# Expert stage of a four-part layer: where the picks are turned, where tile 1 is compared, and how the ranking is dealt over a turn

## The chip, the cores and the metric

The program runs on one core of one Trainium2 chip. The metric is device time in microseconds (us) for one execution. A profiled execution leaves a trace of every instruction on TensorE (PE, with its weight loads as PEld), VectorE (DVE), ScalarE (ACT), GpSimd (POOL) and SyncE (SP). Times in rows count from the start of the profiled span.

## The reference

The input x is 4 batches of 512 tokens of width 256. Four residual updates follow each other: a cross attention with a bias, an attention with gated expert values, a cross attention with layer norm, and a product-key expert layer. The change sits at the seam between the third and the fourth, and in the fourth. Cut to what matters, the fourth is:

```python
def _L1_ffn_ref(x, w_q, keys, expert_down, expert_up, norm_w):      # H=8, DK=128, K=8, NKEYS=64
    xn = _rmsnorm(x, norm_w)
    q = (xn @ w_q.T).reshape(b, t, H, 2, DK)
    sim1 = einsum('bthd,hkd->bthk', q[..., 0, :], keys[:, :, 0, :])
    sim2 = einsum('bthd,hkd->bthk', q[..., 1, :], keys[:, :, 1, :])
    s1, i1 = top_k(sim1, K); s2, i2 = top_k(sim2, K)
    all_idx = i1[..., :, None] * NKEYS + i2[..., None, :]
    all_sc  = s1[..., :, None] + s2[..., None, :]
    fs, pk = top_k(all_sc, K)                                        # 8 heads x 8 picks = 64 picks a token
    fi = take_along_axis(all_idx, pk)
    hidden = gelu(einsum('btd,bthkd->bthk', xn, expert_down[fi])) * relu(fs)
    return einsum('bthk,bthkd->btd', hidden, expert_up[fi])
```

## The kernel before

The kernel is four program blocks, one for each part of the layer. All engines meet at the end of a block, and the next begins when the last of them is done. Inside a block each engine has its own hand-written order of work, and semaphores tie them together.

The expert block (`product_key_experts`) takes the 2048 tokens as 16 tiles of 128. It gathers nothing: all 4096 experts are computed densely, as 128 x 32. For a tile there are these steps.

- ACT normalises the tile (`stage_tile`), PE turns it (`turn_x`, L2379), and ACT takes it out (L2486).
- PE compares it with the folded keys: 8 matmuls of 512 columns (`compare`, L2390). ACT takes the similarities out (`sims`, L2493).
- DVE ranks them in parts. Part 0 is 16 MAX8 (`largest`, L2186) and part 1 the 16 places (`largest_places`, L2282). Parts 2 to 5 (`rank`, L2235 to L2272) add pairs, take the 8 best of each head and work out the expert's row and column.
- PE turns the picks (`turn_picks`, L2400, 12 small matmuls), ACT takes them out (`picks`, L2500 and L2501), and DVE splits the score (`split_score`, L2553 and L2556) into three bf16 parts.
- DVE builds one-hots for the 64 picks in four rounds of 16 (`onehots`, rounds 0 to 3, L2569, L2574, L2580). There are two buffers for them.
- PE computes the hidden values of all experts in 8 blocks of 16 matmuls (`hidden`, L2416), and ACT applies gelu to each (L2509).
- PE sums the one-hots into a dense matrix of weights in 8 blocks of 24 matmuls (`weights`, L2433). DVE multiplies it with the hidden values (`apply`, L2592).
- PE multiplies the product with the up table in 8 blocks of 8 matmuls (`spend`, L2443). DVE adds the result to x (`update`, L2598).

The work is software-pipelined. Turn i runs over blocks n = 0 to 7. In each block PE does `spend` of tile i-1, `hidden` of tile i+1 and `weights` of tile i. In turn i the similarities of tile i+2 are made too, after block 3, and the picks of tile i+1 are turned in block 5. DVE does `apply(i, n)` in each block. Beside it come, in blocks 0 to 3, the ranking of tile i+1 (parts 1, 2, 3, then 4 and 5 together), the last two one-hot rounds of tile i in blocks 1 and 3, MAX8 of tile i+2 in block 5, the split and round 0 of tile i+1 in block 6, and its round 1 in block 7. From turn 2 on, block 4 also holds a small part of a late norm.

PE's waits in a turn are these. `weights(i, n)` with even n waits for one-hot round n/2 of tile i, and from n = 3 on for `apply(i, n-3)`, since three PSUM banks go round. `spend(i-1, 0)` of the next turn waits for the last `apply`. `turn_picks(i+1)` waits for the 43rd ranking step.

Before turn 0, the expert block runs `hidden(0, 2)` to `hidden(0, 7)`, with `turn_x(1)` after the first, `turn_picks(0)` after block 4 and `compare(1)` at the end. Blocks 0 and 1, and the ranking of tile 0, already ran in the attention block before it. Then PE waits for the up table (4 MB, issued by SP at the block's start behind 1 MB of the down table) and for both halves of tile 1's similarities:

```python
                compare(1, 1)
                eng.wait_ge(s["up_loaded"], 16)
                eng.wait_ge(sim_ready.sem, sim_ready.at(1, 2))
```

At the end of the attention block, PE projects four query tiles (L520) and DVE adds each to x (`update`, two instructions, L766 and L769). The fourth goes through PSUM bank 6.

## Time and profile before

| What | Value |
|---|---|
| Median of 3 runs | 2230.97 us (2230.22 to 2232.72) |
| Profiled execution: its own time | 2233.26 us |
| Profiled execution: span | 2231.5 us |
| Mean granted TensorE clock | 0.997 |
| PE busy | 2169.8 us, 97% |
| DVE busy | 1686.2 us, 76% |
| ACT busy | 814.7 us, 37% |
| POOL busy | 177.8 us, 8% |

A row of a timeline gives the start, the duration, the engine, the line, the operation and how many instructions are merged. In brackets stands the engine's idle time before it and what ended that. PE durations are modelled a little long: in a chain without a gap the next group starts about 0.16 us before the printed end. The profiled execution took 2.3 us more than the median of the runs. 1.8 us of its time lie outside the span.

### The profile page before, as it was taken

To read this page: it belongs to the slowest core of one execution; us is meant where nothing else is said; L and a number is where in the kernel's file an instruction comes from. 1 tells how busy PE (TensorE), PEld (TensorE's weight loads), DVE (VectorE), ACT (ScalarE), POOL (GpSimd) and SP (SyncE) were. 2 spreads that over 40 slices of the span, in tenths; PEclk is the share of its full clock that TensorE was granted. 3 is DMA by queue.
4 is the path that set the end of the run, shared out by engine and by line. 5 is a ranking of instruction groups with operands and counts; after the bars stand their busy time and mean duration, and the time that the engine had idled before them with its cause. 6 is when DMAs were issued, how large, how long until landed. Compare 5 with 4: busy or idle time off the path is not lost. (4 is left out here: it accounts for less than half of the span.)

```text
span 2231.5 us, 45916 instructions
## 1 busy us (share of the span) xinstructions
PE 2169.8 (97%) x18243; PEld 1464.3 (66%) x18276; DVE 1686.2 (76%) x4495; ACT 814.7 (37%) x1943; POOL 177.8 (8%) x427
## 2 busy tenths in 40 slices
PE   7999999999999999999999999999989999999998
PEld 3555554446756756775555555556679989898997
DVE  6898896876576576536877787877698989888885
ACT  4888882311312302303554554545322111211110
POOL 4552201000000000000000000000000000000000
PEclk9999999999999999999999999999999999999999
DMA  5011104000000003001000000001200000000000
GB/s 179 24 42 44 28 9 156 1 1 1 1 1 1 1 0 114 1 1 50 2 1 1 1 1 1 1 1 58 95 1 2 2 11 2 1 11 2 1 11 11
DMA packets 24166, 48.65 MB, mean 22 GB/s; under 512 B 5009, under 2 KB 13457, under 8 KB 22929
## 3 DMA queue, kind: packets, MB, share of 16 engines
q1 hardware_dynamic: 23952, 45.71, 6.2%
q8 instruction: 146, 2.39, 0.4%
q14 instruction: 68, 0.55, 0.1%
HBM read 37.57 MB, written 2.10 MB: 18 GB/s over the span
## 5 line engine op out<-in xcount | busy, mean ns | idle before, releaser
L2416 PE MATMUL banks<-work,big 128*128 128x128 f32 x2016 | 248.9, 277 | 2.2 <-PEq L378 1.5
L623 ACT ACTIVATE work<-banks,work 128x512 f32<-128x512 f32 x256 | 174.6, 686 | 202.3 <-DVE work L742 202.3
L2416 PEld LDWEIGHTS banks<-work,big 128*128 128x128 f32 x2016 | 242.3, 193 | 7.8 <-issue 3.4
L1121 PE MATMUL banks<-big,work 128*128 128x256 f32 x1024 | 241.3, 379 | 3.6 <-issue 3.3
L1045 PE MATMUL banks<-big,work 128*128 128x512 f32 x512 | 226.6, 596 | 0.3 <-DMA big<-in_B_val 0.2
L2509 ACT ACTIVATE work<-banks 128x512 f32<-128x512 f32 x126 | 75.2, 597 | 407.4 <-PE banks L2416 404.3
L1121 PEld LDWEIGHTS banks<-big,work 128*128 128x128 f32 x1024 | 195.4, 191 | 33.6 <-issue 1.9
L1939 ACT ACTIVATE work<-work 128x512 f32<-128x512 f32 x256 | 181.0, 711 | 0.0
L1045 PEld LDWEIGHTS banks<-big,work 128*128 128x128 f32 x512 | 95.6, 190 | 114.0 <-issue 112.6
L742 DVE TENSOR_REDUCE work<-banks 128x2 f32<-128x1024 f32 x128 | 150.5, 1218 | 7.7 <-PE banks L475 7.7
L1343 DVE CUSTOM_DVE_ANT_0 work<-banks,work 128x512 f32<-128x512 f32 (+3 forms) x128 | 57.7, 488 | 121.5 <-PE banks L1061 109.2
L1843 PEld LDWEIGHTS banks<-ident,work 64*128 64x128 f32 x2048 | 75.5, 139 | 90.9 <-ACT work L1939 58.7
L1228 ACT ACTIVATE work<-work 128x512 f32<-128x512 f32 (+3 forms) x128 | 70.8, 554 | 168.7 <-DVE work L1343 168.7
L491 PEld LDWEIGHTS banks<-ident,work 64*128 64x128 f32 x2048 | 74.0, 139 | 89.0 <-issue 51.5
L2443 PE MATMUL banks<-big,wab 128*128 128x256 f32 x512 | 126.4, 390 | 3.6 <-DVE wab L2592 3.6
L1312 DVE TENSOR_TENSOR work<-banks,work 128x512 f32<-128x512 f32 x128 | 88.0, 691 | 51.8 <-PE banks L1045 51.3
L475 PE MATMUL banks<-work 64*128 64x256 f32 x1024 | 124.6, 383 | 0.9 <-DVE work L735 0.9
L2443 PE MATMUL banks<-big,work 128*128 128x256 f32 x512 | 123.7, 387 | 0.8 <-DVE work L2592 0.8
L504 PE MATMUL banks<-big,wc 128*64 128x512 f32 x512 | 116.9, 599 | 3.2 <-ACT wc L644 2.9
L760 DVE COPY big<-banks 128x512 f32<-128x512 f32 x128 | 87.7, 685 | 38.9 <-PE banks L491 38.7
L751 DVE TENSOR_SCALAR work<-work 128x512 f32<-128x512 f32 x256 | 113.1, 484 | 4.5
L2433 PEld LDWEIGHTS banks<-wc 128*128 128x128 bf16 x3072 | 107.2, 99 | 13.5 <-issue 5.4
(252 smaller groups left out, 3801.3 us busy)
## 6 DMA issues: line engine op xcount, KB each, us to landing
work<-work SPq DMA_DIRECT2D x152, 32.0 KB, 2.0
big<-in_bias SPq DMA_DIRECT2D x16, 256.0 KB, 4.7
big<-in_B_val SPq DMA_DIRECT2D x8, 512.0 KB, 6.6
big<-in_B_out SPq DMA_DIRECT2D x1, 4096.0 KB, 18.3
big<-in_D_downT SPq DMA_DIRECT2D x4, 1024.0 KB, 5.0
big<-in_D_up SPq DMA_DIRECT2D x1, 4096.0 KB, 15.7
wc<-in_ctxT SPq DMA_DIRECT2D x1, 2048.0 KB, 7.8
wab<-in_L_ffn_w_q SPq DMA_DIRECT2D x1, 2048.0 KB, 9.7
```

The lines of the kernel that those rows point to most:

```text
L475: last = eng.matmul(SB[i][:, j, c * 256:(c + 1) * 256], qT[r, t % 2, qt * P:(qt + 1) * P], kT[r, t % 2, c * 256:(c + 1) * 256], start=True ...
L504: last = eng.matmul(FB[0][j * DK:(j + 1) * DK, :], vtok[:, kt, h * DK:(h + 1) * DK], pT[:, (t % 2 * PAIR + j) * QT + kt, :], start=(kt == ...
L623: eng.activation(prob[:, n % NS * PAIR + j, :], SB[n % 2][:, j, :], ACT.Exp, bias=low[:, n % NS, j:j + 1], accum_out=rowsum[:, n % NS, j:j ...
L742: eng.tensor_reduce(low[:, n % NS, :], SB[n % 2], AX.X, ALU.max, negate=True).then_inc(low_ready.sem, 1)
L751: last = eng.tensor_scalar(one, one, rinv[:, n % NS, j:j + 1], None, ALU.mult)
L1045: last = eng.matmul(value_bank(b, n), xnT[:, kc, t * P:(t + 1) * P], w_val[:, kc, h * EB * DK:(h + 1) * EB * DK], start=(kc == 0), stop=(k ...
L1121: last = eng.matmul(XO[qt // 2][:, qt % 2 * D:(qt % 2 + 1) * D], spread[:, c % NG, qt * P:(qt + 1) * P], w_out[:, c, :], start=False, stop ...
L1312: eng.tensor_tensor(scaled[:, n % NG, :].rearrange("p (k e) -> p k e", e=EB), value_bank(b, n).rearrange("p (k e) -> p k e", e=EB), gm[:, ...
L1939: eng.activation(one, one, ACT.Exp, bias=low[:, n % 2, j:j + 1], scale=-1.0, accum_out=rowsum[:, n // QT % 2, at:at + 1]).then_inc(p_ready, 1)
L2416: last = eng.matmul(HP[n % 2][:, q * P:(q + 1) * P], down[:, (n * NJ + q) * KC + kc, :], xnT[par][:, kc, :], start=(kc == 0), stop=(kc == ...
L2433: last = eng.matmul(dst, hot[:, c, at, :], lot[c][:, at, f, :], start=(f == 0), stop=(f == 2))
L2443: last = eng.matmul(UPP[par][:, 0:D], G[par][:, j, :], up[:, j, :], start=(j == 0), stop=(j == ELO - 1))
```

## The change

In the attention block:

- the fourth `update` leaves DVE's order, and ACT's order ends with `stage_tile(1)`, which used to be ACT's first work in the expert block.

In the expert block, before turn 0:

- PE begins with `turn_picks(0)` and ACT with `picks(0)`;
- `turn_x(1)` stays after `hidden(0, 2)`, and now waits until ACT has taken the picks out;
- `compare(1)` comes after `hidden(0, 4)` and writes banks 2 and 3 in place of 0 and 1, without waiting for a gelu;
- DVE begins with the attention's fourth update (`last_update`), then split and one-hot rounds 0 and 1 of tile 0, then ranking parts 0 and 1 of tile 1.

In the turns:

- `turn_picks(i+1)` and `picks(i+1)` go from block 5 to block 7;
- `weights(i, 0)` is issued in block 1, behind `hidden(i+1, 1)` and right before `weights(i, 1)`;
- the ranking of tile i+1 is dealt as parts 1, 2, 3 in blocks 0, 1, 2, part 4 in block 4 and part 5 in block 5 (in turn 0, where part 1 is done: parts 2, 3, 4, 5 in blocks 0, 2, 4, 5);
- MAX8 of tile i+2 goes from block 5 to 6; the split and both one-hot rounds of tile i+1 come together after `apply(i, 7)`.

```diff
@@ c_attention
                 start_gelu(eng, m, 1)
+                stage_tile(eng, m, 1)
...
                 update(B - 1, 2, FB[1])
-                update(B - 1, 3, FB[0])
@@ product_key_experts, tensor
                     eng.wait_ge(staged.sem, staged.at(i, 1))
+                    if i == 1:
+                        eng.wait_ge(selt_ready.sem, selt_ready.at(0, 2))
...
-                    if i:
-                        before = (i - 1, SELECT + 1) if i >= 2 else (0, NB)
-                        eng.wait_ge(h_ready.sem, h_ready.at(*before))
+                    if i >= 2:
+                        eng.wait_ge(h_ready.sem, h_ready.at(i - 1, SELECT + 1))
...
+                turn_picks(0)
                 for n in range(2, NB):
                     hidden(0, 0, n)
                     if n == 2:
                         turn_x(1)
-                    if n == START_PICK:
-                        turn_picks(0)
-                compare(1, 1)
+                    if n == SELECT + 1:
+                        compare(1, 1)
...
                         if n == PICK and ahead >= 1:      # PICK 5 -> 7
                             turn_picks(i + 1)
-                        if n != SELECT + 1:
+                        if n == 1:
+                            weights(i, 0)
+                        if n and n != SELECT + 1:
                             weights(i, n)
@@ scalar
-                stage_tile(eng, m, 1)
+                picks(0)
                 for n in range(2, NB):
                     hidden(0, 0, n)
-                    if n == START_PICK:
-                        picks(0)
-                select(1, 1)
+                    if n == 2:
+                        take_x(1, 1)
+                    if n == SELECT + 1:
+                        take_sims(1)
@@ vector
+                def last_update():
+                    eng.wait_ge(c_out.sem, c_out.at(B - 1, QT))
+                    eng.tensor_tensor(c_y, bank[6][:, 0:D], c_bo, ALU.add).then_inc(c_added, 1)
+                    eng.wait_ge(c_added, 1)
+                    xt = x[:, NT - 1, :]
+                    eng.scalar_tensor_tensor(out=xt, in0=c_y, scalar=m["gates"][:, 5:6], in1=xt, op0=ALU.mult, op1=ALU.add
+                                             ).then_inc(c_added, 1)
+                last_update()
                 split_score(0)
                 onehots(0, 0)
                 onehots(0, 1)
                 topk(1, 0)
+                topk(1, 1)
+                PARTS = {0: 1, 1: 2, 2: 3, 4: 4, 5: 5}
+                FIRST_PARTS = {0: 2, 2: 3, 4: 4, 5: 5}
...
-                        if ahead >= 1 and n < 4:
-                            topk(i + 1, n + 1)
+                        parts = PARTS if i else FIRST_PARTS
+                        if ahead >= 1 and n in parts:
+                            topk(i + 1, parts[n])
...
-                        if ahead >= 2 and n == PICK:
+                        if ahead >= 2 and n == PICK - 1:
                             topk(i + 2, 0)
-                        if ahead >= 1 and n == PICK + 1:
+                        if ahead >= 1 and n == PICK:
                             split_score(i + 1)
                             onehots(i + 1, 0)
-                        if ahead >= 1 and n == NB - 1:
                             onehots(i + 1, 1)
```

## Rows read from the trace of the kernel before

**Rows 1.** Windows: length, busy (count) of PE, PEld, DVE, ACT, POOL; PEclk, DMA, GB/s.

```profile
1636.00:1648.00 12.00, 8.66 (x123) 8.57 (x124) 9.37 (x36) 2.18 (x5) 0.00 (x0) 0.86 0.00 1
...
1687.00:1726.00 39.00, 39.00 (x414) 34.84 (x413) 34.44 (x125) 7.50 (x15) 0.00 (x0) 1.00 0.01 2
...
2190.00:2198.00 8.00, 6.19 (x48) 5.22 (x49) 5.85 (x6) 0.00 (x0) 0.00 (x0) 0.79 0.01 2
```

**Rows 2.** PE's waits in the expert stage: us in total, times, longest.

```profile
PE banks L2400 <- DVE work L2272: 5.3, 2, 4.2
PE banks L2443 <- DVE wab L2592: 3.6, 2, 1.9
```

**Rows 3.** Timeline of PE, from the block's start to turn 0.

```profile
1598.18 2.02 PE L2416 MATMUL banks<-work,big 128*128 128x128 f32 x16 [1.45 <-PEq L378]
...
1603.92 0.57 PE L2400 MATMUL banks<-ident,work 128*64 128x64 f32 x12
1604.43 5.62 PE L2416 MATMUL banks<-work,big 128*128 128x128 f32 x48
1611.26 3.70 PE L2390 MATMUL banks<-work 128*128 128x512 f32 x8 [1.20 <-ACT work L2486]
1615.69 2.02 PE L2416 MATMUL banks<-work,big 128*128 128x128 f32 x16 [0.73 <-issue]
```

**Rows 4.** Timeline of PE, end of turn 0 and start of turn 1.

```profile
1639.34 0.57 PE L2400 MATMUL banks<-ident,work 128*64 128x64 f32 x12 [4.20 <-DVE work L2272]
...
1647.23 2.03 PE L2416 MATMUL banks<-work,big 128*128 128x128 f32 x16
1650.97 2.00 PE L2443 MATMUL banks<-big,wab 128*128 128x256 f32 x8 [1.71 <-DVE wab L2592]
```

**Rows 5.** Timeline of PE, three groups of a later turn.

```profile
1689.78 2.00 PE L2443 MATMUL banks<-big,work 128*128 128x256 f32 x8
1691.61 0.86 PE L2433 MATMUL banks<-wc 128*128 128x64 bf16 x24
1692.31 1.97 PE L2443 MATMUL banks<-big,work 128*128 128x256 f32 x8
```

**Rows 6.** Timeline of PE, turns 14 and 15.

```profile
2179.99 0.57 PE L2400 MATMUL banks<-ident,work 128*64 128x64 f32 x12 [1.05 <-DVE work L2272]
...
2191.81 2.91 PE L2443 MATMUL banks<-big,wab 128*128 128x256 f32 x8 [1.85 <-DVE wab L2592]
...
2212.84 0.86 PE L2433 MATMUL banks<-wc 128*128 128x64 bf16 x24
2214.48 14.08 PE L2443 MATMUL banks<-big,work 128*128 128x256 f32 x64 [0.78 <-DVE work L2592]
```

**Rows 7.** Timeline of DVE, from the last update of the attention block on.

```profile
1597.23 0.48 DVE L769 SCALAR_TENSOR_TENSOR x<-work,gates,x 128x256 f32<-128x256 f32 x1
1605.17 0.23 DVE L2553 CAST work<-work 128x128 bf16<-128x128 f32 x1 [7.46 <-ACT work L2501]
...
1606.53 0.69 DVE L2569 TENSOR_TENSOR wc<-work,wc 128x1024 bf16<-128x1024 bf16 x1
...
1609.94 0.69 DVE L2569 TENSOR_TENSOR wc<-work,wc 128x1024 bf16<-128x1024 bf16 x1
...
1626.25 0.68 DVE L2235 TENSOR_TENSOR wab<-work 128x512 f32<-128x512 f32 x1
...
1635.02 0.42 DVE L2223 TENSOR_TENSOR wab<-work 128x512 bf16<-128x512 bf16 x1
...
1639.19 0.68 DVE L2592 TENSOR_TENSOR wab<-banks,work 128x512 f32<-128x512 f32 x1
...
1642.09 1.98 DVE L2186 MAX8 work<-work 128x8 f32<-128x64 f32 x15
```

**Rows 8.** Timeline of SP: the up table's issue.

```profile
1598.36 0.42 SPq L2355 DMA_DIRECT2D big<-in_D_up  x1
```

**Rows 9.** DMA issues of that stretch: KB, us from issue to landing.

```profile
big<-in_D_up SPq DMA_DIRECT2D x1, 4096.0 KB, 15.7
```

More of the change, by code:

```diff
@@ L145, in build @@
         m["A.dve_took"] = sem("A_dve_took")
+        m["C.out_made"] = Signal(nc, ctx, "C_out_made", QT)
         m["B.spent"] = Signal(nc, ctx, "B_spread_used", B_.groups * EB)
@@ L365, in c_attention @@
         av_made, on_ready = sig("av_made", T), sig("onorm_ready", T)
-        out_made, y_ready, turn_done = sig("out_made", QT), sig("y_ready", QT), sig("x_updated", QT)
+        out_made, y_ready, turn_done = m["C.out_made"], sig("y_ready", QT), sig("x_updated", QT)
         norm, e = m["C.norm"], m["D"]
@@ L2322, in product_key_experts @@
     gate = m["gates"][:, 3:4]
+    c_out, c_y, c_bo = m["C.out_made"], m["work"][:, 15616:15872], m["work"][:, 15872:16128]
     every_other = ident.rearrange("p (n two) -> p two n", two=2)
-    SELECT, PICK, START_PICK = 3, 5, 4
+    SELECT, PICK = 3, 7
     late, LATE, LATE_FROM = e.norm, 4, 2
@@ L2332, in sem @@
             return ctx.enter_context(nc.semaphore("D_" + what))
-        consts = sem("consts")
+        consts, c_added = sem("consts"), sem("last_attention_added")
         staged, xt_made, xt_ready, sim_made, sim_ready, step = e.staged, e.xt_made, e.xt_ready, e.sim_made, e.sim_ready, e.step
@@ L2384, in compare @@
                     eng.wait_ge(xt_ready.sem, xt_ready.at(i, 1))
-                    if i:
-                        before = (i - 1, SELECT + 1) if i >= 2 else (0, NB)
-                        eng.wait_ge(h_ready.sem, h_ready.at(*before))
+                    if i >= 2:
+                        eng.wait_ge(h_ready.sem, h_ready.at(i - 1, SELECT + 1))
                     for n in range(2):
                         for kc in range(KC):
-                            last = eng.matmul(HP[n][:, :], xnT[par][:, kc, :], simw[:, kc, n * 512:(n + 1) * 512],
+                            last = eng.matmul(WP[n] if i == 1 else HP[n][:, :], xnT[par][:, kc, :], simw[:, kc, n * 512:(n + 1) * 512],
                                               start=(kc == 0), stop=(kc == KC - 1))
@@ L2482, in _, with take_x @@
             def _(eng):
-                def select(i, par):
+                def take_x(i, par):
                     eng.wait_ge(xt_made.sem, xt_made.at(i, 1))
@@ L2488, in select, with take_sims @@
                     last.then_inc(xt_ready.sem, 1)
+                def take_sims(i):
                     for n in range(2):
@@ L2493, in select @@
                         eng.activation(sims[:, n * HD:(n + 1) * HD, :],
-                                       HP[n][:, :].rearrange("p (a b) -> p a b", b=NK), ACT.Copy).then_inc(sim_ready.sem, 1)
+                                       (WP[n] if i == 1 else HP[n][:, :]).rearrange("p (a b) -> p a b", b=NK), ACT.Copy).then_inc(sim_ready.sem, 1)
                 def picks(i):
@@ L2525, in turn @@
                         if ahead >= 2 and n == SELECT:
-                            select(i + 2, par)
+                            take_x(i + 2, par)
+                            take_sims(i + 2)
                         if ahead >= 1 and n == PICK:
@@ L2545, in topk @@
                         rank(eng, m, i, part, selt_made)
-                    if part == 4:
-                        rank(eng, m, i, 5, selt_made)
                 def split_score(i):
@@ L2612, in turn @@
                             update(i - 2, par)
-                        if ahead >= 1 and n < 4:
-                            topk(i + 1, n + 1)
+                        parts = PARTS if i else FIRST_PARTS
+                        if ahead >= 1 and n in parts:
+                            topk(i + 1, parts[n])
                         if n == LATE and LATE_FROM <= i < LATE_FROM + late.parts:
+                            if i == LATE_FROM:
+                                eng.wait_ge(c_added, 2)
                             late.on_vector(eng, B - 1, i - LATE_FROM)
-                        if ahead >= 2 and n == PICK:
+                        if ahead >= 2 and n == PICK - 1:
                             topk(i + 2, 0)
-                        if ahead >= 1 and n == PICK + 1:
+                        if ahead >= 1 and n == PICK:
                             split_score(i + 1)
                             onehots(i + 1, 0)
-                        if ahead >= 1 and n == NB - 1:
                             onehots(i + 1, 1)
```

## The prediction

> **What bounds the kernel now.** I read the windows first. In a whole steady turn PE is busy for 39.00 of 39.00 us at clock 1.00, while DVE is busy for 34.44 us [rows 1]. So the turns from 1 to 13 are bound by PE, and moving work among DVE's slots there can gain nothing. It can only lose. The change removes no matmul. What it can win is idle PE time, so the next view is PE's waits, and there only the first and the last turns count: the picks waited for ranking (L2400 for DVE L2272) 5.3 us in two places, and the first `spend` of a turn for `apply` 3.6 us in two places [rows 2]. The timeline places them: 4.20 us before the picks of tile 1 and 1.71 us before the first `spend` of turn 1 [rows 4], 1.05 and 1.85 us in turns 14 and 15 [rows 6]. At the block's start there are three more: 1.45 us between the blocks, 1.20 us before `compare(1)` and 0.73 us before turn 0 [rows 3].
>
> Two of these waits cost more than their length. Around the 4.20 us the granted clock averaged 0.86 over 12 us, so part of it ran at 1.2 instead of 2.4 GHz: 0.14 x 12 = 1.7 us lost. Around the 1.85 us it was 0.79 over 8 us: another 1.7 us [rows 1, 6]. After 1.71 us idle the `spend` took 2.00 us [rows 4], as in a turn without a wait [rows 5], so that one cost only itself.
>
> **Block start.** The attention block now ends with PE, not with DVE's fourth update. DVE ended at 1597.23 + 0.48 = 1597.71, and PE began 0.47 us later, at 1598.18 [rows 3, 7]. PE itself had ended at 1598.18 - 1.45 = 1596.73 [rows 3]. With the same 0.47 us the stage starts at 1597.2, 1.0 us earlier. The two instructions of the update (about 1 us) now lie on DVE at the block's start, where DVE was idle for 7.46 us [rows 7]. `stage_tile(1)` lies on ACT, idle during the last projections. Both cost nothing.
>
> **From there to turn 0.** PE issues the picks (0.51 us, from 1603.92 to 1604.43), then blocks 2 to 4 with `turn_x` in between (5.74 us, from 1598.18 to 1603.92), `compare(1)` (3.70 us printed, less the 0.16 us by which groups overlap: 3.54), then blocks 5 to 7 (5.62 less 0.16, about 5.5) [rows 3]. The new wait of `turn_x(1)` for ACT's copies is covered by `hidden(0, 2)`, 1.87 us against about 0.6 us of copies behind the picks; behind it would queue only PE. `compare(1)` has `hidden(0, 3)` and `hidden(0, 4)` between it and ACT's copy, so the 1.20 us wait goes, and blocks 5 to 7 lie between it and turn 0, so the 0.73 us goes. PE is through at 1597.2 + 0.51 + 5.74 + 3.54 + 5.5 = 1612.5.
>
> What is late next is the up table. Its DMA was issued at 1598.36 and took 15.7 us [rows 8, 9]: landed at 1614.1, hidden behind the wait that ended at 1615.69. Issued 1.0 us earlier, it lands at 1613.1. Its cost is a wait of 0.6 us. So turn 0 begins at 1613.1 against 1615.69 [rows 3]: **gain 2.6 us**. Bounds: 3.2 if the table is not late, 1.6 if it lands no earlier than before.
>
> The Trainium skill, "DMA: Bandwidth & Descriptors", section "Measured", gives 341 GB/s for 1 MB and 425 GB/s for 16 MB, issued from GpSimd. An estimate from it for the two transfers, 5.2 MB at some 400 GB/s, is 13 us: the table would be in time, and the total would be 0.6 us better. The row says 15.7 us, and I go by the row.
>
> **Turn 0.** It lasted 1647.23 - 1615.69 = 31.54 us [rows 3, 4]. Without the 4.20 us wait and the 1.7 us of slow clock it is 25.6 us. The question is whether DVE now delivers the picks by then. PE reaches them, before `weights(0, 7)`, at 25.6 - 0.51 - 0.70 = 24.4 us into the turn. DVE enters the turn with parts 0 and 1 of tile 1 done: the last one-hot round of tile 0 ends near 1597.2 + 1.2 (copies) + 1.36 + 2 x 3.41 = 1606.6; tile 1's similarities are there near 1607.9, and parts 0 and 1 take 2.1 and about 3.1 us, to 1613.2, before the first `apply` can start. That is what the move of `compare(1)` buys. `apply(0, 0)` starts behind two hidden blocks and one block of weights, 2 x 1.87 + 0.86 + 0.1 = 4.7 us in. From there to the end of part 5 there are parts 4 and 5, 1639.19 - 1635.02 = 4.17 us; parts 2 and 3, which are the 8.77 us from 1626.25 to 1635.02 less two `apply` of 0.68 and one one-hot round of 3.41, 4.00 us; two one-hot rounds, 6.82 us; and six `apply`, 4.1 us [rows 7]. Sum 19.1, so the picks are ready 23.8 us in, 0.6 us before PE asks. The 4.20 us and its clock loss go: **gain 5.9 us**. The margin is thin: beyond it each us late costs one.
>
> **Start of turn 1.** `spend(0, 0)` needs `apply(0, 7)`. DVE has `apply(0, 6)` and the MAX8s of tile 2 (about 2.1 us [rows 7]) in front: 23.8 + 0.7 + 2.1 + 0.7 = 27.3 us into turn 0. PE gets there at 25.6 + 1.87 = 27.5. The 1.71 us go [rows 4]: **gain 1.7 us**. Before, a split and one-hot round lay in front of that `apply`; they now lie behind it.
>
> **The steady turns.** No gain, and a cost of nothing if the new chain fits. Let P be the start of `turn_picks(i+1)`. `weights(i, 7)` starts at P + 0.51, and `apply(i, 7)` ends at about P + 2.1 (0.51, then 1.64 us from a block of weights to the `spend` behind its `apply` [rows 6]). Split and one-hot round 0 then take 1.36 + 3.41 [rows 7]: ready at P + 6.9. PE asks for it in `weights(i+1, 0)`, behind `weights(i, 7)`, two hidden and two spend blocks: P + 0.51 + 0.70 + 2 x 1.87 + 2 x 1.83 = P + 8.6 [rows 3, 5]. Slack 1.7 us. Moving `weights(., 0)` back by one block makes that slack; without it there would be none. DVE's extra work in turns 2 to 9 (a part of the norm) falls in block 4, before it waits for block 5. Ranking ends some 4 us before the picks, as the turn has 4.5 us of free DVE time [rows 1].
>
> **Turns 14 and 15.** Turn 14 has no compare and so asks for the picks 3.5 us sooner, but block 7 is two blocks later than block 5: the 1.05 us go. In turn 15 there are no hidden blocks to hide the chain. After `weights(14, 7)` the first `spend` waits 0.8 us, as the last one does [rows 6], against 1.85. Then `spend(14, 0)` and `(14, 1)` end at P + 2.1 + 2 x 1.83 = P + 5.8, and `weights(15, 0)` waits until P + 6.9: a new wait of 1.1 us. `weights(15, 2)` waits for round 1 (3.41 us later, P + 10.3) and PE is there at P + 6.9 + 1.4 + 1.83 = P + 10.1: 0.2 us. New waits 2.1, old 1.05 + 1.85 + 1.7 of slow clock = 4.6: **gain 2.5 us**, if the clock holds.
>
> The row of 1.85 us idle shows a fall of the clock, that of 1.71 us none [rows 4, 6]. Here there are three short waits close together, and whether they count as one, no row says. Bounds: 0 and 1.7 us. I take 0, because none is longer than 1.71 us. The Trainium skill, "TensorE: Matmul & The Clock Gate", section "What's actually happening", says that the clock follows how busy TensorE has been recently, with the slow state as the default. That speaks against the change at this place: by it the scattered waits could add up to the same fall, and the total gain would be 11.0 us instead of 12.7.
>
> **Sum.** 2.6 + 5.9 + 1.7 + 2.5 = 12.7 us. Of the profiled execution, 2233.26 us, that leaves 2220.6; it stands 2.3 us above the median of the runs, so for the median 2230.97 - 12.7 = **2218.3 us**, 0.57% faster.
>
> **Rivals.**
>
> - *The change works, but part is given back:* the clock falls in turn 15 (1.7 us), or the thin margins of 0.6 us in turn 0 and 0.2 us in turn 1 are missed by 1 to 3 us. For it speaks that both margins are smaller than what I had to estimate without a row (ACT's copies, waking times). 2220 to 2224 us.
> - *Turn 0 stays bound by DVE:* if DVE could not use the earlier start (parts 0 and 1 not done before the first `apply`), the picks wait and the `spend` wait come back. Only the block start and the end are left, 5.1 us: 2225.9. Against it: the 7.46 us in which DVE was idle before the split [rows 7], and now fills.
> - *A wait in every turn, and slower:* the one-hots of the next tile start only after `apply(i, 7)`, and the first weights of each turn stand behind them. If that chain (picks, ACT, DVE, weights) is later than I count by more than its slack of 1.7 us, each further us costs 15 us over 15 turns. From 2.5 us late on it eats the whole gain; at 3.5 us late it gives 2230.97 - 12.7 + 15 x 1.8 = 2245 us. For it: DVE has three more things in a row there than before. Against it: every duration in the chain is from a row, and none varies.
> - *Nothing changes:* the waits only move, to the up table or to the attention block's end. The table would have to land 5 us later than before to take even half of the gain, and nothing is put in front of it. 2229 to 2232 us.
>
> **How the numbers follow.** My forecast, 2216 to 2220 us, has a chance of 0.68; the first rival 0.18; DVE-bound turn 0 0.04; a wait in every turn 0.07, of which 0.05 ends slower; nothing 0.03. About 0.2% (4.5 us) is what a measurement of this kernel can tell from no change, so faster means under 2226.5: 0.68 + 0.18 + 0.04 = 0.90, same 0.05, slower 0.05. The range takes in the forecast with its bounds (0.6 better with the table in time, 1 for the spread of runs) and the first rival: 2216 to 2223.
>
> **What would show it.** In the profile after: PE's first group near 1597.2 and it is the picks; turn 0 starts near 1613.1, behind a short wait for a DMA; no wait of PE for L2272 anywhere; turn 0 of 25.6 us; steady turns without a gap in PE, as before; in turn 15 waits of about 0.8, 1.1 and 0.2 us, and the clock there near 1.00. A wait of `weights` for the one-hot rounds (L2580) in each turn, or gaps of PE in the steady turns, would make the forecast wrong.

## The result, and the profile after

The changed kernel takes 2214.26 us (median of 4 runs, 2212.79 to 2215.63). Beside it the kernel before took 2230.59 us (4 runs, 2230.01 to 2232.72). The ratio is 0.9925, with an interval of 0.9908 to 0.9942: 16.3 us faster. The direction was as forecast, the size was not. The forecast was 2218.3 us, 12.7 us less, and its range began at 2216, 1.7 us above the measured median. The same change, timed again beside the experiments of the third batch, gave 0.9919 (0.9905 to 0.9932). By both intervals the gain is more than the 12.7 us forecast (0.9942 of 2230.59 us is 12.9 us less).

The profiled execution of the changed kernel took 2212.79 us with a span of 2211.0 us, 20.5 us less than the span before. Of these, 3.0 us arise ahead of the expert stage, in parts that the change doesn't touch: in the profiles of this study the projections of the attention block end anywhere from 1593.7 to 1598.5 us. I therefore compare stage with stage, from the end of PE's last projection (start of PE's first group in the expert block less the idle time printed there) to the start of the last 64 `spend` matmuls. Before that is 1596.73 to 2214.48 [rows 3, 6], 617.75 us. After it is 1593.73 to 2193.99, 600.26 us. The gain inside the stage is **17.5 us**. Behind it lie 17.0 us in both.

The timeline of PE after, from the block's start to the second block of turn 1:

```profile
1594.05 0.57 PE L2403 MATMUL banks<-ident,work 128*64 128x64 f32 x12 [0.32 <-PEq L379]
1594.55 2.05 PE L2419 MATMUL banks<-work,big 128*128 128x128 f32 x16
...
1600.23 3.60 PE L2393 MATMUL banks<-work 128*128 128x512 f32 x8
1603.66 5.52 PE L2419 MATMUL banks<-work,big 128*128 128x128 f32 x48
1609.84 3.84 PE L2419 MATMUL banks<-work,big 128*128 128x128 f32 x32 [0.66 <-DMA big<-in_D_up]
...
1634.30 0.57 PE L2403 MATMUL banks<-ident,work 128*64 128x64 f32 x12
1634.81 0.87 PE L2436 MATMUL banks<-wc 128*128 128x64 bf16 x24
1635.52 2.03 PE L2419 MATMUL banks<-work,big 128*128 128x128 f32 x16
1637.38 3.62 PE L2446 MATMUL banks<-big,wab 128*128 128x256 f32 x16
```

The same view at turn 2, turns 13 and 14, and the end:

```profile
1674.00 2.03 PE L2419 MATMUL banks<-work,big 128*128 128x128 f32 x16
1675.87 3.62 PE L2446 MATMUL banks<-big,work 128*128 128x256 f32 x16
...
2097.32 2.03 PE L2419 MATMUL banks<-work,big 128*128 128x128 f32 x16
...
2135.80 2.03 PE L2419 MATMUL banks<-work,big 128*128 128x128 f32 x16
...
2171.63 3.72 PE L2446 MATMUL banks<-big,wab 128*128 128x256 f32 x16 [0.78 <-DVE wab L2599]
...
2176.38 1.57 PE L2436 MATMUL banks<-wc 128*128 128x64 bf16 x48 [1.03 <-DVE wc L2587]
...
2193.99 14.08 PE L2446 MATMUL banks<-big,work 128*128 128x256 f32 x64 [0.78 <-DVE work L2599]
```

All waits of PE in the expert stage after (us in total, times, longest), against the long ones of [rows 2]:

```profile
PE banks L2436 <- DVE wc L2587: 1.0, 1, 1.0
PE banks L2446 <- DVE wab L2599: 0.8, 1, 0.8
PE banks L2446 <- DVE work L2599: 0.8, 1, 0.8
PE banks L2393 <- ACT work L2491: 0.7, 1, 0.7
PE banks L2419 <- DMA big<-in_D_up: 0.7, 1, 0.7
PE banks L2403 <- PEq L379: 0.3, 1, 0.3
```

The reader is to see three things. The picks (L2403) at 1634.30 and the first `spend` at 1637.38 have no bracket any more. A new short bracket stands ahead of turn 0, for the up table. And from one turn's start to the next, 2097.32 to 2135.80, there are 38.48 us, where a turn before took 38.81 (1687.77 to 1726.58 in the rows of the next section). The stage, split at the same points in both traces (turns counted from their first `hidden` group):

| Stretch | before, us | after, us | gain | forecast |
|---|---|---|---|---|
| Projections' end to turn 0 | 18.96 | 16.11 | 2.85 | 2.6 |
| Turn 0 | 31.54 | 25.68 | 5.86 | 5.9 |
| Turn 1, its start to its first `spend` | 3.74 | 1.86 | 1.88 | 1.7 |
| From there to the start of turn 14 | 502.51 | 498.42 | **4.09** | **0** |
| Turn 14 to the last `spend` | 61.00 | 58.19 | 2.81 | 2.5 |
| Sum | 617.75 | 600.26 | 17.49 | 12.7 |

Four terms are within about 0.3 us of their forecast. The whole miss is one row: 13 steady turns, for which the prediction said "No gain".

### The profile page after: what moved, and what is told of

The parts are those of the page before. It is cut to its first block and busy times, and to the rows that moved or that the text cites. A ratio compares the mean times of both kernels' runs of the same rounds, so it can differ in the third digit from the quotient of the medians.

```text
span 2211.0 us, 45960 instructions
## 1 busy us (share of the span) xinstructions
PE 2163.5 (98%) x18276; PEld 1457.6 (66%) x18276; DVE 1685.3 (76%) x4495; ACT 815.0 (37%) x1943; POOL 178.9 (8%) x427
## 5 line engine op out<-in xcount | busy, mean ns | idle before, releaser
L2587 DVE TENSOR_TENSOR wc<-wc,work 128x3072 bf16<-128x3072 bf16 x64 | 112.1, 1751 | 0.0
## 6 DMA issues: line engine op xcount, KB each, us to landing
big<-in_D_up SPq DMA_DIRECT2D x1, 4096.0 KB, 15.4
```

The lines of the kernel that those rows point to most:

```text
L2587: eng.tensor_tensor(lot[b].rearrange("p n f (j two) -> p n f j two", two=2), elo[:, b].rearrange("p n (j two) -> p n j two", two=2).unsque ...
```

## Why the steady turns became shorter

Before, PE had no printed idle time in a steady turn [rows 1], and [rows 5] show none ahead of the first `spend`. But a `hidden` group and that `spend` started 2.01 us apart before and 1.86 us after. The weight loads of the kernel before, at that same `spend`, tell why. First three of PE's rows of the kernel before, then its weight loads (PEld), then DVE:

```profile
1687.77 2.03 PE L2416 MATMUL banks<-work,big 128*128 128x128 f32 x16
...
1713.17 1.89 PE L2443 MATMUL banks<-big,work 128*128 128x256 f32 x8
...
1726.58 2.03 PE L2416 MATMUL banks<-work,big 128*128 128x128 f32 x16
```

```profile
1689.78 1.59 PEld L2443 LDWEIGHTS banks<-big,work 128*128 128x128 f32 x8 [0.17 <-DVE work L2592]
...
1692.28 1.60 PEld L2443 LDWEIGHTS banks<-big,work 128*128 128x128 f32 x8
```

```profile
1689.04 0.69 DVE L2592 TENSOR_TENSOR work<-banks,work 128x512 f32<-128x512 f32 x1
```

The last `apply` of the turn ended at 1689.04 + 0.69 = 1689.73, and 0.05 us later PE loaded the weights that `apply` had made. The load waited 0.17 us, and the matmul that follows it started in the same instant, 1689.78 [rows 5]. As the printed ends of matmuls are modelled about 0.16 us late, that wait disappears in PE's own rows: the engine is printed as 100% busy. One sign is left in PE's rows: this `spend` is printed with 2.00 us [rows 5], where one behind a `hidden` group, with no wait, is printed with 1.89 (1713.17 above). After the change the loads run ahead of the matmul, as they do elsewhere. PEld and DVE after:

```profile
1675.76 3.33 PEld L2446 LDWEIGHTS banks<-big,work 128*128 128x128 f32 x16
```

```profile
1674.20 0.69 DVE L2599 TENSOR_TENSOR work<-banks,work 128x512 f32<-128x512 f32 x1 [2.17 <-PE banks L2436]
```

`apply` ends at 1674.89, the load starts at 1675.76, and the matmul at 1675.87, 0.11 us behind its load. The wait is worth 0.15 us (2.01 less 1.86), and the first `spend` behind it, whose loads had no lead, took 1.83 against 1.73 us: 0.10. Together 0.25 us a turn. The reason is DVE's order: before, the split and round 0 stood ahead of `apply(i, 7)`; now they stand behind it.

The other 0.08 us of the 0.33: `weights(i, 0)` and `weights(i, 1)` now follow each other, so PE goes 7 times a turn from a bf16 `weights` group to an fp32 group, not 8. In the trace after, `hidden` behind `weights` takes 1.86 us to the next group (2.03 printed), behind `spend` 1.78 (1.95 printed). These are two readings of a trace; experiments 2, 3 and 9 test them.

The experiments below call this 0.08 us a change from bf16 to fp32, but the rows of the loads point to something else: it too is a load that starts late. Behind `weights` the load of an fp32 group starts 0.03 us ahead of its matmul (1692.28 above, for the `spend` at 1692.31 in [rows 5]), behind `hidden` 0.11 us ahead. A `spend` then takes 1.81 or 1.73 us to the next group: 0.08 us less lead, 0.08 us more time. The two leads are each the length of one matmul of the group before, 0.70 / 24 = 0.03 us for `weights` and 1.78 / 16 = 0.11 us for `hidden`. And there is a loss without a change of type: in the kernel before, the fp32 `hidden` matmuls behind the fp32 picks (1604.43) have a load that starts in the same instant, and 48 of them are printed with 5.62 us [rows 3]; after, behind `compare`, 48 are printed with 5.52 us (1603.66 above), both at clock 1.00:

```profile
1604.43 5.44 PEld L2416 LDWEIGHTS banks<-work,big 128*128 128x128 f32 x48
```

All bf16 groups of this kernel are also those with the short matmuls of 64 columns, so no run here separates the type from the length.

## The experiments

Ten kernels, and the change once more, were run in three batches. Each batch had its own runs of the kernel before: 2230.39, 2230.68 and 2231.83 us. "Stage" is the length defined above; the change has 600.3 in both of its profiles. Line numbers shift by a few between the kernels. The stage is read from one profile of each kernel; it repeats well, with 600.26, 600.31, 600.35 and 600.32 us for the change, its second profile and the kernels of experiments 5 and 8. The medians of whole executions are coarser: each interval is about 3 us wide to either side, and the change itself was timed beside the third batch only. So differences of 1 to 2 us among the kernels below rest on the stage.

**1. `weights(i, 0)` back in block 0.**

```diff
-                        if n == 1:
-                            weights(i, 0)
-                        if n and n != SELECT + 1:
+                        if n != SELECT + 1:
                             weights(i, n)
```

> The changed kernel with one thing undone: weights(i, 0) is issued in block 0 of each turn again, behind the first spend, and not in block 1. Theory 1 (the chain picks, ACT's copies, split, one-hot round 0 is ready 6.85 us after the picks start, as the trace of the changed kernel shows, and PE asks for it there): PE would ask 0.51 + 0.71 + 1.86 + 1.73 = 4.8 us after the picks start, so each turn from 1 to 14 gains a wait of about 2.05 us before weights(i, 0) for L2587, the steady turn goes from 38.49 to about 40.6 us, and the time to about 2214 + 14 x 2.1 = 2243 us, slower than the kernel before. Theory 2 (DVE has free time in a turn and catches up, so the order on PE is indifferent): within 2 us of the changed kernel, 2212 to 2217 us.

Measured: 2253.55 us (2250.68 to 2254.55), ratio 1.0104 (1.0088 to 1.0119): slower. The waits of PE, and one of the places in its timeline:

```profile
PE banks L2436 <- DVE wc L2585: 30.0, 15, 2.8
```

```profile
1761.65 1.89 PE L2446 MATMUL banks<-big,work 128*128 128x256 f32 x8
1765.48 0.87 PE L2436 MATMUL banks<-wc 128*128 128x64 bf16 x24 [1.94 <-DVE wc L2585]
1766.19 1.97 PE L2446 MATMUL banks<-big,work 128*128 128x256 f32 x8
```

It is the wait that the third rival of the prediction described, 15 times, and issuing `weights(i, 0)` one block later is what avoids it: the stage is 637.7 us here, 37.4 longer. The time is more than theory 1 gave. A turn without a fall of the clock takes 40.68 us, 2.20 more than 38.48 where about 2.1 was expected: 1.94 printed, 0.16 by which printed idle time is short, and one more change from bf16 to fp32. In three of the turns the granted clock fell after the wait (0.96 mean over the 41 us of one such turn, about 1.6 us lost), in the other turns an equal wait left it at 1.00; and the wait of turn 15 was 2.76 us, longer than any of these and without a fall (clock 1.00 over the 10 us around it).

**2. Split before the last `apply`.** `split_score(i + 1)` ahead of `apply(i, 7)`, which puts about 1.4 us of DVE back before it.

```diff
                     for n in range(NB):
+                        if ahead >= 1 and n == PICK:
+                            split_score(i + 1)
                         apply(i, par, n)
...
                         if ahead >= 1 and n == PICK:
-                            split_score(i + 1)
                             onehots(i + 1, 0)
```

> The changed kernel with the split of the score put before the last apply of each turn on DVE, so that this apply ends about 1.4 us later. Theory 1 (in the kernel before, the first spend of every turn waited for that apply, about 0.15 to 0.25 us, though no gap is printed): the apply now ends near P + 3.24 (P the start of the picks) and the spend, free to start at P + 3.08, starts near P + 3.3; the steady turn goes from 38.49 to 38.7 to 38.8 us, close to the 38.81 of the kernel before, and the time rises by 3 to 5 us. Theory 2 (the 0.33 us a turn come only from the two blocks of weights standing side by side, and no wait is hidden): the steady turn stays at 38.49 us and the time rises by under 1 us, in turn 0 alone.

Measured: 2217.74 us (2214.81 to 2218.51), ratio 0.9939 (0.9926 to 0.9953); stage 602.3, 2.0 longer. From turn 1's first `spend` to turn 14 it takes 500.29 us against 498.42, 0.14 a turn; the first `spend` of turn 1 comes 0.45 later, and turns 14 and 15 give 0.26 back. Again PE prints no gap, and again the loads show it (PE, PEld, DVE of this kernel):

```profile
1674.80 2.03 PE L2419 MATMUL banks<-work,big 128*128 128x128 f32 x16
1676.71 3.72 PE L2446 MATMUL banks<-big,work 128*128 128x256 f32 x16
```

```profile
1676.71 3.32 PEld L2446 LDWEIGHTS banks<-big,work 128*128 128x128 f32 x16
```

```profile
1675.97 0.68 DVE L2599 TENSOR_TENSOR work<-banks,work 128x512 f32<-128x512 f32 x1
```

`apply` ends at 1676.65, load and matmul both start at 1676.71, 0.06 later. The `spend` starts 1.91 us behind the `hidden` where it was 1.86, and the two blocks of `spend` take 3.56 instead of 3.46. A load that loses its lead costs 0.10 even where the matmul itself is only 0.05 late. Theory 1 holds, in a smaller size, since `apply` ends a little earlier here than before the change: 1.85 us behind the start of the `hidden` group, against 1.96. This experiment brings back 0.14 of the 0.25 us; the other 0.11 are read from those 1.96 us and were not put back by a run.

**3. The two weight blocks apart.** `weights(i, 1)` behind `spend(i-1, 2)`, so 8 changes from bf16 to fp32 in a turn again.

```diff
                         if i:
                             spend(i - 1, 1 - par, n)
+                        if n == 2:
+                            weights(i, 1)
...
-                        if n and n != SELECT + 1:
+                        if n > 1 and n != SELECT + 1:
                             weights(i, n)
```

> The changed kernel with weights(i, 1) moved behind spend(i-1, 2), so that the two blocks of weights are no longer side by side, while the first spend and the first weights stay where they are. Theory 1 (most of the 0.33 us a turn is a hidden wait of the first spend, only about 0.08 us is the change between fp32 and bf16 matmuls): steady turn about 38.57 us, time up by about 1 us. Theory 2 (the 0.33 us are all from standing side by side): steady turn about 38.8 us, time up by 4 to 5 us.

Measured: 2217.01 us (2213.92 to 2217.23), ratio 0.9935 (0.9922 to 0.9949); stage 601.4, 1.2 longer. The steady part takes 499.50 us, 0.083 a turn more. That is the 0.08 of theory 1, and with the 0.25 read above it makes up the 0.33.

**4. The seam undone.** The fourth `update` and `stage_tile(1)` at their old places.

```diff
                 start_gelu(eng, m, 1)
-                stage_tile(eng, m, 1)
...
                 update(B - 1, 2, FB[1])
+                update(B - 1, 3, FB[0])
...
+                stage_tile(eng, m, 1)
                 picks(0)
...
-                last_update()
                 split_score(0)
```

> The changed kernel with the seam undone: the attention's fourth update is again DVE's last work in the attention block, and stage_tile(1) is ACT's first in the expert block. Theory 1 (the block starts when its last engine is done, and the up table then bounds the start of turn 0): the expert block starts 1.0 us later after PE's last projection, turn 0 too, and the time rises by about 1.0 us. Since turn_x(1) waits for staging and for the picks' copies, nothing else moves. Theory 2 (the update hides, as its cost is taken from the waits before turn 0): the wait for the up table shrinks and the time stays within 0.3 us.

Measured: 2215.91 us (2212.47 to 2216.65), ratio 0.993 (0.9916 to 0.9943); stage 601.3, 1.0 longer. PE's first row:

```profile
1597.86 0.57 PE L2403 MATMUL banks<-ident,work 128*64 128x64 f32 x12 [1.30 <-PEq L379]
```

1.30 us between the blocks where the change has 0.32: the 1.0 us of the prediction. The wait for the table stays at 0.7, since its issue moves along with the block's start.

**5. `compare(1)` late.** At its old place behind `hidden(0, 7)`, and ACT's `take_sims(1)` with it; the banks as in the change.

```diff
                 for n in range(2, NB):
                     hidden(0, 0, n)
                     if n == 2:
                         turn_x(1)
-                    if n == SELECT + 1:
-                        compare(1, 1)
+                compare(1, 1)
```

> The changed kernel with compare(1) put back to the end of the block's start, behind hidden(0, 7), still in banks 2 and 3. Theory 1 (the early comparison buys almost nothing where it stands: PE waits for the up table anyway, and DVE can use its similarities only to be 0.6 us ahead of the first apply): PE's order is as long as before, the similarities are there about when the up table is, MAX8 and places end 0.6 us after the first apply could start, the picks still come in time, and the time is that of the changed kernel within 0.5 us. Theory 2, that of the prediction (the move of compare(1) is what lets DVE deliver the picks in time): a wait for L2273 before the picks of tile 1 comes back, 2 us or more, with a fall of the clock, and the time rises by 2 to 6 us.

Measured: 2213.71 us (2212.81 to 2215.02), ratio 0.9925 (0.9912 to 0.9939); stage 600.35, the same. In DVE's timeline here tile 1's first MAX8 comes 5.3 us later than in the change (1604.50 there), and the first `apply` 0.6 us later (1614.49 there, behind 4.62 us idle):

```profile
1609.79 0.22 DVE L2187 MAX8 work<-work 128x8 f32<-128x64 f32 x1 [6.32 <-issue]
...
1615.07 0.67 DVE L2597 TENSOR_TENSOR wab<-banks,work 128x512 f32<-128x512 f32 x1
```

Even so the picks come at 1634.32 without a wait. That part of the change buys nothing here, where PE waits for the up table ahead of turn 0 in any case (0.75 us).

**6. The whole block start undone, the turns as in the change.** Experiment 4, and the order of PE, ACT and DVE before turn 0 as before, with all five ranking parts in turn 0.

```diff
-                turn_picks(0)
                 for n in range(2, NB):
                     hidden(0, 0, n)
                     if n == 2:
                         turn_x(1)
-                    if n == SELECT + 1:
-                        compare(1, 1)
+                    if n == 4:
+                        turn_picks(0)
+                compare(1, 1)
...
-                topk(1, 1)
-                FIRST_PARTS = {0: 2, 2: 3, 4: 4, 5: 5}
+                FIRST_PARTS = PARTS
```

> The changed kernel with the whole block start as in the kernel before (fourth update and staging at their old places, picks of tile 0 after block 4, compare(1) last, ranking part 1 of tile 1 inside turn 0); the turns are those of the change. Theory 1 (the stage is the sum of its parts): 2.85 us from the start, and in turn 0 DVE has 3.1 us more to do, so that the picks come about 26.5 us into the turn against 24.4: a wait of about 2.1 us, 0.3 us at the next spend, and perhaps 1.6 us of half clock. Time 5 to 7 us above the changed kernel, about 2219 to 2221 us; steady turn 38.49 us. Theory 2 (the later picks and weights alone remove the waits of turn 0): 2.9 us above. Theory 3 (the waits of turn 0 come back in full): 10 us above.

Measured: 2222.30 us (2219.12 to 2222.74), ratio 0.996 (0.9946 to 0.9973); stage 605.6, 5.3 longer. So the edits in the turns alone bring 12.2 of the 17.5 us, and those at the start, on top of them, 5.3: 2.85 ahead of turn 0, 2.2 for the picks in turn 0, and 0.3 behind them. PE at the picks of tile 1, and the window around them:

```profile
1643.62 0.57 PE L2402 MATMUL banks<-ident,work 128*64 128x64 f32 x12 [2.13 <-DVE work L2273]
```

```profile
1634.00:1650.00 16.00, 13.87 (x169) 13.05 (x168) 15.55 (x46) 3.97 (x8) 0.00 (x0) 1.00 0.01 2
```

2.13 us idle, and the granted clock (1.00, the column behind POOL's) stayed at 2.4 GHz.

**7. Half of the up table early.** 2 MB of the table are issued in the attention block, behind the last but one head pair's product (the expectation says sixth-last, which is a slip), and 2 MB at the expert block's start. `turn_x` and `take_x` in the turns go one block earlier.

```diff
+                eng.wait_ge(av_made.sem, av_made.at(B - 1, T - 1))
+                eng.dma_start(d_views(m)[2][:, :ELO // 2, :], a["D.up"][:, :ELO // 2, :]).then_inc(s["up_loaded"], 16)
...
-                        if n == SELECT and ahead >= 2:
+                        if n == SELECT - 1 and ahead >= 2:
                             turn_x(i + 2)
```

> The changed kernel with two things added: the first half of the up table (2 MB) is fetched from the attention block as soon as its half of the buffer is free, behind the sixth-last head pair's product, and turn_x(i+2) with ACT's copy stands one block earlier in a turn. Theory 1 (the two waits that the trace of the changed kernel still shows at these places, 0.66 us for the table and 0.72 us before compare(2), are real and nothing is late behind them until 1.3 us): both waits go, the picks and the first spend of turn 1 become late by 0.1 to 0.2 us, and the time falls by 1.1 to 1.5 us. Theory 2 (DVE's margins in turn 0, 0.97 us before the picks, take it back): the time falls by under 0.7 us.

Measured: 2213.31 us (2211.36 to 2214.52), ratio 0.992 (0.9906 to 0.9933); stage 598.7, 1.6 shorter, and both waits of 0.7 us (the table, and `compare` in turn 0 for ACT) are gone from the list. The two halves took 8.7 us each to land (median):

```profile
big<-in_D_up SPq DMA_DIRECT2D x2, 2048.0 KB, 8.7
```

**8. Ranking not dealt.** Parts 1, 2, 3 and 4 with 5 in blocks 0 to 3, as before the change.

```diff
-                PARTS = {0: 1, 1: 2, 2: 3, 4: 4, 5: 5}
-                FIRST_PARTS = {0: 2, 2: 3, 4: 4, 5: 5}
+                PARTS = {0: 1, 1: 2, 2: 3, 3: 4}
+                FIRST_PARTS = {1: 2, 2: 3, 3: 4}
...
                         rank(eng, m, i, part, selt_made)
+                    if part == 4:
+                        rank(eng, m, i, 5, selt_made)
```

> The changed kernel with the ranking dealt as before: parts 1, 2, 3, then 4 and 5 together, in blocks 0 to 3 (in turn 0 parts 2, 3, then 4 and 5, in blocks 1 to 3). Theory 1 (with the picks in block 7, DVE's order between the applies has slack, and dealing the ranking over the blocks does nothing): no new wait, time within 0.5 us of the changed kernel. Theory 2 (parts 4 and 5 together hold up apply(i, 4), and weights of blocks 6 and 7 wait for it): a wait of PE for L2599 in each turn, some 1 us each, 10 us or more in all.

Measured: 2213.59 us (2213.13 to 2217.56), ratio 0.9923 (0.9909 to 0.9936); stage 600.3, the same waits. Dealing the ranking over the blocks does nothing here.

**The change again.** The kernel of the change as it stands, as the mark for the third batch.

> The changed kernel once more, for the comparison with the next two in one set of runs. By all theories: 2213 to 2215 us, steady turn 38.49 us, and 600.3 us from the end of the last projection to the start of the last spend.

Measured: 2213.68 us (2212.66 to 2215.89), ratio 0.9919 (0.9905 to 0.9932); stage 600.3.

**9. All blocks of a turn in pairs.** PE's order in a turn: two `spend`, two `hidden`, two `weights`, so 4 changes from bf16 to fp32 instead of 7. Ranking part 4 goes to block 3 and MAX8 to block 5, to fit.

```diff
-                    for n in range(NB):
...
+                    for n in range(0, NB, 2):
+                        if i:
+                            spend(i - 1, 1 - par, n)
+                        if n == SELECT + 1 and ahead >= 2:
+                            compare(i + 2, par)
+                        if i:
+                            spend(i - 1, 1 - par, n + 1)
+                        if n and ahead >= 1:
+                            hidden(i + 1, 1 - par, n)
+                        if ahead >= 1:
+                            hidden(i + 1, 1 - par, n + 1)
+                        weights(i, n)
+                        weights(i, n + 1)
```

> The changed kernel with all blocks of a turn taken in pairs on PE (two spends, two hidden, two weights; the comparison between the spends of blocks 4 and 5), ranking part 4 in block 3 and MAX8 in block 5 so that DVE is in time. Theory 1 (each change from bf16 to fp32 matmuls costs PE 0.08 us, and three more of them go in each turn): steady turn 38.49 - 0.25 = 38.24 us, and the time falls by 3 to 3.6 us. Theory 2 (the 0.08 us belong to the first pair alone, or the gain returns as waits for apply or for one-hot rounds, which now come later by a block): steady turn 38.4 us or more, the time within 1 us or above.

Measured: 2211.89 us (2208.88 to 2213.13), ratio 0.9906 (0.9891 to 0.9921); stage 596.5, 3.8 shorter. A turn of it, from start to start:

```profile
1638.80 2.03 PE L2419 MATMUL banks<-work,big 128*128 128x128 f32 x16
...
1677.04 2.03 PE L2419 MATMUL banks<-work,big 128*128 128x128 f32 x16
```

38.24 us, 0.24 less than 38.48: three changes of 0.08. Of the 3.8 us, 3.2 lie in the steady turns and 0.7 in the last two. The median fell by 1.8 us only, where 3 to 3.6 were expected; in the profile, the part ahead of the stage ended 2.3 us later than in that of the change beside it, and the stage is what the edit acts on.

**10. Pairs, and half of the table early.** Experiments 7 and 9 together; the diff is that of both, with one difference: `turn_x` stands between the two `hidden` groups of a pair.

> The pairs of blocks together with the early half of the up table and the earlier turn_x. Theory 1 (the gains add until DVE bounds turn 0): steady turn 38.24 us; the waits for the table and before compare(2) are gone, and the picks of tile 1 wait about 0.7 us; time 4 to 4.7 us below the changed kernel, about 2209.5 us. Theory 2 (in turn 0 DVE takes all of it back): 3 us below, as the pairs alone.

Measured: 2209.21 us (2208.20 to 2210.97), ratio 0.9899 (0.9884 to 0.9914); stage 595.9. It beats both kernels: 22.6 us under the kernel before and 4.5 us under the change, of the same batch. The two gains don't add up in full (4.4 us against 1.6 + 3.8). About half of what is missing lies in the steady turns: they take 38.29 us, and not the 38.24 that was expected. In experiment 9 the short `turn_x` stands behind `weights` and loses 0.03 us there, and the `spend` behind it loses nothing; here the `spend` stands behind `weights` and loses 0.08. The other half, 0.4 us, lies ahead of turn 1, where a wait of the picks comes back, because turn 0 now starts earlier than DVE can follow:

```profile
1633.15 0.57 PE L2405 MATMUL banks<-ident,work 128*64 128x64 f32 x12 [0.89 <-DVE work L2275]
```

## Why the prediction was right in its direction and too small

**The step that failed** is the first conclusion from [rows 1]: "moving work among DVE's slots there can gain nothing", and with it "No gain" for the steady turns. PE printed as busy for 39.00 of 39.00 us was taken as proof that it waited for nothing. It waited 0.15 us in every turn and loaded late for another 0.10, on an `apply` that the change moves ahead of the split; experiment 2 brings 0.14 of these 0.25 back by moving the split alone. The prediction even used the sign of that wait as proof of its absence: it found the `spend` after 1.71 us idle as long as one "in a turn without a wait", 2.00 us, but the latter, of [rows 5], was the one that waited unseen. The 0.08 us for a `weights` group followed by an fp32 group was there in the trace before (one and the same `hidden` group is printed with 1.95 or 2.03 us) and was put at nothing in the sum; experiment 3 measures it alone. Together they gave 4.09 us up to turn 14, and 0.33 more inside the last stretch.

**Start to turn 0, 2.6 forecast, 2.85 measured.** Between the blocks 1.13 us went instead of 1.0; experiment 4 shows that the seam is worth 1.0. PE's first group was the picks, as said. The up table became late, as said: a wait of 0.66 us against the forecast 0.6. It took 15.4 us to land, against 15.7 [rows 9]. The estimate from the Trainium skill, "DMA: Bandwidth & Descriptors", section "Measured", 13 us, does not agree with this trace: its table is for transfers issued from GpSimd and gives the time in which the DMA engines are busy, while the 15.4 us here count from SP's issue to landing. The row was the better guide.

**Turn 0, 5.9 forecast, 5.86 measured.** The agreement is partly luck. Counted from where picks start when nothing holds them (3.74 us behind the start of the two `hidden` groups at 1631.31), the wait was 4.3 us, not the printed 4.20, and the slow clock cost 1.55 us (1.27 and 2.86 us for two groups that take 0.71 and 1.87 otherwise), not 1.7; the two errors nearly cancel. DVE ended the ranking 0.97 us ahead of the picks, where 0.6 was forecast. But one reason given was wrong. The sentence on the early similarities, "That is what the move of `compare(1)` buys", falls with experiment 5: with `compare(1)` late, the first `apply` comes 0.6 us later, and the slack of 0.97 takes that up. What counts is that parts 0 and 1 lie ahead of turn 0 at all; when all of the block start is undone, the picks wait 2.13 us (experiment 6, in which part 1 is again inside turn 0, among other things).

**Start of turn 1, 1.7 forecast, 1.88 measured.** `apply(0, 7)` ended at 1636.56 and the `spend` came at 1637.38: a margin of 0.8 us where 0.2 was forecast. The 0.17 us beyond the printed 1.71 are the same reading error in small: printed idle time counts from the modelled end of the group before, some 0.16 us late.

**Turns 14 and 15, 2.5 forecast, 2.8 measured,** of which 0.33 are turn 14's share of the shorter turns. The waits were 0.78, 1.03 and none visible, against 0.8, 1.1 and 0.2. The clock held, as I took it to. The window of these waits (clock 1.00 behind POOL's column), against 0.79 in [rows 1]:

```profile
2168.00:2178.00 10.00, 8.19 (x115) 7.11 (x114) 6.95 (x12) 1.01 (x3) 0.00 (x0) 1.00 0.01 2
```

The rule of the Trainium skill, "TensorE: Matmul & The Clock Gate", section "What's actually happening", that the clock follows how busy TensorE has recently been, was put at 1.7 us, for the case that the scattered waits add up. Here they did not.

**The chain of the steady turns** fitted its slack, which was 1.5 us and not 1.7 (round 0 was ready at P + 6.85, as said, and PE asked at P + 8.3, not 8.6), and experiment 1 shows that it had to: with the slack taken away the kernel is 1% slower than before. This was the rival on the other side, and it was rightly built; `weights(i, 0)` one block later decides it.

**The first rival** (part is given back) did not occur in any of its parts. Both thin margins came out larger than forecast, 0.97 for 0.6 and 0.8 for 0.2 us.

## What to carry to other kernels

When an engine is printed as 100% busy, look at its weight loads before calling a stage bound by it: a load with a bracket, or one that starts in the same instant as its matmul, stands for a wait that the matmul rows hide. Here such a wait cost 0.25 us in each turn; with the 0.08 of the order of groups it was 4.1 of the 17.5 us gained. A value that is made just in time already costs; order the engine that makes it so that it ends before the load wants it, and move the latest of its other consumers back, here by one block. Where the waits allow it, put groups of short matmuls side by side, so that fewer long groups follow a short one and start with a late load: this was tried here with bf16 groups of 64 columns ahead of fp32 ones (8, 7 and 4 times a turn), and with no others.

## What the runs showed of the hardware that was not expected

- An fp32 group behind a `weights` group (bf16, 64 columns) took 0.08 us longer than behind fp32 `hidden` or `spend`: 8, 7 and 4 such changes a turn gave 38.57, 38.48 and 38.24 us. Its weight load started 0.03 us ahead of its matmul there, 0.11 us behind `hidden`; with no lead at all a `spend` took 0.10 us longer. So the time follows the lead of the load; whether type or length of the matmuls in front sets that lead is open.
- Idle time alone did not decide the clock. 1.85 us lowered it in the kernel before [rows 1, 6]; 2.13 us in experiment 6 did not; and in experiment 1 equal waits of 1.94 to 1.95 us lowered it in three turns and left it in the others, and 2.76 us left it too. Why is open; no run here separates it from what PE did before the wait.
- The part ahead of the changed code ended up to 5 us apart from one execution to another, with nothing different in it. What causes that was not looked into. It is why stages were compared here, and not only whole spans.
